# Graph-network kernel: the pairwise stage works in place in the adjacency ring, with 14 slots waited for one by one

## The chip, the cores and the metric

One Trainium2 chip; the kernel runs on one of its cores. The metric is device time in microseconds (us) of one execution, the median over the runs. The times below are from a profiled execution unless a median is named.

## What is computed

Four graph-network layers, each `x = x + f(relu(layernorm(x)), adj)`, for 8 graphs ("batches") of 2048 nodes with 128 features; `adj` is 2048 x 2048 for each. Layer 1 is the one that the change touches:

```python
mask = where(adj > 0, 0, -1e22)
q = feat @ W1.T                                  # 2048 x 64
k = feat @ W2.T                                  # 2048 x 64
e = relu(q[:, None, :, :] + k[:, :, None, :])    # for every pair of nodes, 64 values
scores = einsum('bijd,d->bij', e, a)
att = softmax(scores + mask, axis=-1)
return att @ feat
```

Layer 0 is a three-layer graph convolution, layer 2 attention with four heads, layer 3 a normalised product with the adjacency.

## The kernel before, in words

The five engines' programs are written out by hand: each has its own instruction stream with explicit semaphore waits. The batches run one after the other, and in each the four layers one after the other. The pairwise stage is layer 1.

**A tile and its steps.** The stage has 16 tiles per batch (`tile1`); tile t gives the score rows of 128 nodes. A tile has NS = 15 steps. A step has four "column groups" g = 0..3, and for each of them one slot of the buffer `E` (128 x 2048, float32) is filled: either by DVE (`first`, L881, or `second`, L879), or by ACT (`second`, L611). In steps 4, 6, 8 and 12 one slot is "fused": DVE fills it first and adds a second part to it last (L889). Which engine fills what is fixed by `PLAN`: in a tile, DVE writes 34 slots and makes 4 additions, ACT writes 26 slots. When both engines are done with a step (`e_dve`, `e_act`), PE multiplies the four slots by a window of signs into four PSUM banks (L1361, 32 matmuls for a step) and raises `e_used` by one. The scores of a tile are whole in PSUM after step 14. Tiles alternate between two halves of PSUM, u = t % 2.

**The tail of a tile** runs inside the steps of the next tile, at places fixed in each engine's program:
- DVE, after its step 1: `min1` (L904) waits for the last `e_used` of the tile, adds the mask to the scores, takes the row minimum, and writes the sum to `T1`. After it, DVE waits for its own result (`t1_rdy`, L908) and raises `ring_free` (L910).
- ACT, after its step 3: `exp1` (L616), in place in `T1`.
- PE, after step 5: 16 transposes of `T1` (L1272).
- ACT and DVE, after their step 7: `evac1`, PSUM to `PT1`, two chunks each (L523, L915). `PT1` is another name for `HW`, a buffer of the other layers.
- PE, after step 9: `out1`, the product with the features (128 matmuls, L1376).
- DVE, after its step 11: `finish1`, a reciprocal (L921) and, when `out1` is done, the addition to X (L925); after step 12 `stats2` (L983), after step 13 `mask1_tile` (L896, the mask of the tile made in place from its adjacency) and `aggr2` (L988).

In tiles 5, 9 and 13 there is more: DVE normalises four row blocks after steps 3 to 6 (L996), PE makes four transposes after step 12 (L1414). These are called feature tiles below.

**Slots.** `E` has 12 slots, three steps of four. An engine that begins step n of a batch waits once, for `e_used` of step n - 3.

**The adjacency ring.** `ring` has two places of 128 x 2048. SP loads the adjacency rows of tile k into place k % 2 (L404). For tile k of the pairwise stage it waits for `ring_free`, raised by `min1` of tile k - 2 (L427); for the first two tiles of layer 2 for `min1` of tiles 14 and 15 (L433). SP's queue is in order.

**After the stage** (tile 15 has no next tile) its tail is mixed with the first products of layer 2 (`fill`, `low`, `high`), and `mask2` (L1005) makes the masks of layer 2 from the ring.

Of the kernel before, what the change touches and what calls it, by code (L numbers as in the profile page):

```python
# [52 lines left out]
STEPS = NT * HEADS  # L53


EQ = 3
FUSED = (4, 8, 6, 12)
NS = 2 * SETS - 1
SCALAR_TWO = tuple(k for k in range(NS) if k != 1)
# [28 lines left out]
PLAN = tile_plan()  # L88


def e_slot(t, k):

    return 4 * ((t * NS + k) % EQ)


def k_col(t, g, m):
# [74 lines left out]
def build(nc, x, adj, Ws, bs, gammas, betas, W1, W2, a_vec, Wq, bq, Wk, bk, Wv, bv, Wo, bo, Bw, out):  # L171
# [4 lines left out]
    with ExitStack() as ctx:  # L176
# [73 lines left out]
        with ExitStack() as ph:  # L250
            A = sb("adj_res", [P, NT, N], where=ph)
        with ExitStack() as ph:
            E = sb("E", [P, 4 * EQ, N], where=ph)
            QA = sb("QA", [P, N], where=ph)
            QB = sb("QB", [P, N], where=ph)
            T1 = sb("T1", [P, N], where=ph)
            KLO = sb("KLO", [P, N // GR], where=ph)
            KHI = sb("KHI", [P, N // GR], where=ph)
            KBN = sb("KBN", [P, N // GR], where=ph)
            KBP = sb("KBP", [P, N // GR], where=ph)  # L260
# [4 lines left out]
            T2 = sb("T2", [P, 2, HEADS, N], where=ph)  # L265
            PT2 = sb("PT2", [P, 2, HEADS, CH], where=ph)

        PT1 = HW
        ps = ctx.enter_context(nc.psum_tensor("ps", [P, 8, CH], F32))


# [14 lines left out]
        xn_relu = sem("xn_relu")  # L286
        adj_in = [sem("adj_in0"), sem("adj_in1")]
        ring_in = [sem("ring_in0"), sem("ring_in1")]
        ring_free = sem("ring_free")
        dve_self = sem("dve_self")  # L290
        pool_self = sem("pool_self")
        ln_stats = sem("ln_stats")
# [76 lines left out]
        def _(sp):  # L369
# [48 lines left out]
            for b in range(NB):  # L418

                sp.wait_ge(out_done, b * 16 + 16)  # L420
                for t in range(NT):
                    sp.dma_start(X[:, t, :], x_v[bass.ds(b, 1), :, t].rearrange("o p d -> p (o d)")).then_inc(x_in, 16)
                for k in range(NT):
                    if k < 2 and b:
                        sp.wait_ge(at3_ps, (b * NT + k - 1) * NC)
                    else:
                        sp.wait_ge(ring_free, b * NT + k + 1)  # L427
                    if k == 1:
                        sp.wait_ge(deg_rdy, (b + 1) * NT)
                    load_ring(b, k)  # L430
                for k in range(NT):
                    if k < 2:
                        sp.wait_ge(ring_free, b * NT + NT + k + 1)  # L433
                    else:
                        sp.wait_ge(t2_rdy, b * STEPS + (k - 1) * HEADS)
                    load_ring(b, k)
                    if k == 2:
                        stack_queries(b, 2)
                    if 2 <= k < NT - 1:
                        stack_queries(b, k + 1)  # L440
                for k in range(NT):
                    if k < 2:
                        sp.wait_ge(t2_rdy, b * STEPS + (NT + k - 1) * HEADS)
                    else:
                        sp.wait_ge(at3_ps, (b * NT + k - 1) * NC)
                    load_ring(b, k)
                sp.wait_ge(o3_rdy, b * NT + (2 * NT + 3))
                sp.dma_start(out_v[bass.ds(b, 1)].rearrange("o p t d -> p (o t) d"),
                             X[:, :, :]).then_inc(out_done, 16)
# [71 lines left out]
        def _(act):  # L521
# [80 lines left out]

            def step1(b, t, k):

                n = t * NS + k
                if n >= EQ:
                    act.wait_ge(e_used, b * NT * NS + n - EQ + 1)
                for g, (kind, m, by_act) in enumerate(PLAN[k]):
                    if by_act:
                        col = k_col(t, g, m)  # L610
                        last = nc.scalar.activation(E[:, e_slot(t, k) + g, :], QB[:, :], ACT.Relu, bias=KBP[:, col:col + 1])  # L611
                last.then_inc(e_act, 1)

            def exp1(T, u):
                act.wait_ge(t1_rdy, T + 1)
                nc.scalar.activation(T1[:, :], T1[:, :], ACT.Exp, bias=nmin1[:, u:u + 1], scale=-1.0,  # L616
                                     accum_out=rsum1[:, u:u + 1]).then_inc(p1_rdy, 1)

            def evac1(T, u):
                for g in range(2):  # L620
                    act.wait_ge(pt1_ps, T * NC + g + 1)
                    last = evac(PT1[:, g * CH:(g + 1) * CH], ps[:, 4 * u + g, :])
                last.then_inc(pt1_act, 1)

            def tile1(b, t, u, tail):
# [103 lines left out]
        def _(dve):  # L729
# [5 lines left out]
                own.wait(dve, b)  # L735


            nc.vector.memset(s_win[:, :], 0.0).then_inc(ring_free, 1)
            nc.vector.memset(mv[:, :, :], 0.0).then_inc(ring_free, 1)
            for buf in (stats[:, :, :], dinv[:, :], rstd[:, :]):  # L740
                nc.vector.memset(buf, 0.0).then_inc(cleared, 1)
            dve.wait_ge(ring_free, 2)
            dve.wait_ge(cleared, 3)
            dve.sem_inc(o3_rdy, NT + 3)
            dve.wait_ge(out_done, 16)
            dve.wait_ge(const_in, 16 * CONST_DMAS)
# [119 lines left out]

            def step1(b, t, k):

                n = t * NS + k
                if n >= EQ:  # L870
                    dve.wait_ge(e_used, b * NT * NS + n - EQ + 1)
                add = None
                for g, (kind, m, by_act) in sorted(enumerate(PLAN[k]), key=lambda x: x[1][0] != "fused"):
                    if by_act:
                        continue
                    col = k_col(t, g, m)
                    dst = E[:, e_slot(t, k) + g, :]
                    if kind == "second":
                        last = nc.vector.tensor_scalar(dst, QB[:, :], KBN[:, col:col + 1], None, ALU.max)  # L879
                    else:  # L880
                        last = nc.vector.tensor_scalar(dst, QA[:, :], KLO[:, col:col + 1], KHI[:, col:col + 1], ALU.max, ALU.min)  # L881
                    if kind == "fused":
                        last.then_inc(e_first, 1)
                        add = dst, col
                if add:
                    dst, col = add
                    at = [j for j, row in enumerate(PLAN) if any(kind == "fused" for kind, _, _ in row)].index(k)
                    dve.wait_ge(e_first, (b * NT + t) * 4 + at + 1)
                    last = nc.vector.scalar_tensor_tensor(out=dst, in0=QB[:, :], scalar=KBN[:, col:col + 1], in1=dst,  # L889
                                                          op0=ALU.max, op1=ALU.add)  # L890
                last.then_inc(e_dve, 1)
# [7 lines left out]
            def min1(T, u):  # L899

                dve.wait_ge(e_used, (T + 1) * NS)
                dve.wait_ge(mask1, T + 1)
                alone(dve)
                nc.vector.tensor_tensor_reduce(  # L904
                    out=T1[:, :], in0=ps[:, 4 * u:4 * u + 4, :].rearrange("p c n -> p (c n)"), in1=ring[:, u, :],
                    scale=1.0, scalar=BIG, op0=ALU.add, op1=ALU.min, accum_out=nmin1[:, u:u + 1]
                ).then_inc(t1_rdy, 1)
                dve.wait_ge(t1_rdy, T + 1)  # L908

                dve.sem_inc(ring_free, 1)  # L910

            def evac1(T, u):
                for g in range(2, 4):
                    dve.wait_ge(pt1_ps, T * NC + g + 1)
                    last = nc.vector.tensor_copy(PT1[:, g * CH:(g + 1) * CH], ps[:, 4 * u + g, :])  # L915
                last.then_inc(pt1_dve, 1)

            def finish1(t, T, u):
# [9 lines left out]
            def tile1(b, t, u, tail):  # L928
# [3 lines left out]
                for k in range(NS):  # L932
# [4 lines left out]
                        min1(T - 1, 1 - u)  # L937
                    if tail and k == 7:
                        evac1(T - 1, 1 - u)
                    if tail and k == 11:  # L940
                        finish1(t - 1, T - 1, 1 - u)
                    if k == 13:
                        mask1_tile(b, T, t // 2, u)
                    if t in (5, 9, 13) and 3 <= k < 7:
                        normal2(b, t // 4 - 1, (t - 8 + k,))
                    if tail and k == 12:
                        stats2(b, t - 1)
                    if tail and k == 13:
                        aggr2(b, t - 1)

# [310 lines left out]
        def _(pe):  # L1261
# [85 lines left out]
            def step1(b, t, k, u):  # L1347
# [6 lines left out]
                    pe.wait_ge(x2_rdy, T - 1)  # L1354
                if k == 0 and t in (6, 10, 14):
                    pe.wait_ge(ht_sb, b * (HTS * NC) + NC + t // 4)
                s = e_slot(t, k)
                for c in range(NC):
                    for g, (kind, m, by_act) in enumerate(PLAN[k]):
                        win = s_win[:, QROWS - GR - GR * m:2 * QROWS - GR - GR * m]  # L1360
                        last = mm(ps[QROWS * g:QROWS * (g + 1), 4 * u + c, :], win,  # L1361
                                  E[:, s + g, c * CH:(c + 1) * CH], start=(k == 0), stop=(k == NS - 1),
                                  tile_position=(0, QROWS * g))
                last.then_inc(e_used, 1)

            def probs_t1(T, u):
                pe.wait_ge(p1_rdy, T + 1)
                transposes(lambda t: T1[:, t * P:(t + 1) * P], 4 * u, pt1_ps)

            def out1(T, u):  # L1370
                pe.wait_ge(pt1_act, T + 1)
                pe.wait_ge(pt1_dve, T + 1)
                for j in range(NT):
                    for g in range(NC):
                        rows = slice(QROWS * g, QROWS * (g + 1))
                        last = mm(ps[rows, 4 * u, 0:D], PT1[:, j * P + QROWS * g:j * P + QROWS * (g + 1)], H[:, j, :],  # L1376
                                  start=(j == 0), stop=(j == NT - 1), tile_position=(0, QROWS * g))
                last.then_inc(o1_ps, 1)

# [223 lines left out]
```

## Time and profile before

| | |
|---|---|
| median of 3 runs | 12219.96 us (12218.97 to 12223.52) |
| profiled execution, its own time | 12227.2 us |
| its span | 12225.4 us |
| busy: PE, DVE, ACT | 97%, 84%, 76% |
| DMA, mean over the span | 50 GB/s |
| granted TensorE clock | 0.996 of full speed |

The profile is one execution. Busy time is given for each engine; "idle before" of a group of instructions is the time in which their engine stood still just before them, with what released it. The chain of waits follows the last instruction back to what released it, and so on to the start. A batch takes some 1510 us; its pairwise stage lies, for the second batch, about from 1816 to 2714 us of the span. A matmul's end is modelled; its start is recorded.

### The profile page before, as it was taken

What the parts mean: (1) busy time and instruction counts of PE and PEld (TensorE: products, weight loads), DVE (VectorE), ACT (ScalarE), POOL (GpSimd) and SP (SyncE); (2) the same over time, 40 slices, a digit from 0 to 9 for tenths busy, and PEclk for the clock granted to TensorE, in tenths of its full rate; (3) what the DMA queues carried; (4) which work ended last, traced back from release to release, by engine and by line L of the source; (5) the groups of instructions that cost most, each with busy time, mean ns of one, the idle gap of its engine ahead of it and who ended that gap; (6) DMA issues with size and microseconds to landing.
All of it is one profiled execution on the core that took longest, in us unless ns stands there. A gap on an engine that the chain in (4) does not pass through costs nothing.

```text
span 12225.4 us, 264459 instructions
## 1 busy us (share of the span) xinstructions
PE 11903.6 (97%) x118401; PEld 5910.8 (48%) x118401; DVE 10279.6 (84%) x12373; ACT 9349.5 (76%) x7633; POOL 459.0 (4%) x636
## 2 busy tenths in 40 slices
PE   7999999999999999999999999999999999999999
PEld 3333853338433384333843348433484334843348
DVE  4999849998599975999759997599975999759997
ACT  3998739987499874988748987489874898749986
POOL 1000000000000000000000000000000000000000
PEclk9999999999999999999999999999999999999999
DMA  2000320003200031000310003100031000410013
GB/s 75 19 22 22 107 79 22 19 22 115 74 19 19 26 120 66 19 19 27 130 55 19 19 28 136 48 19 19 31 139 42 19 22 31 141 37 19 22 32 106
DMA packets 206183, 611.30 MB, mean 50 GB/s; under 512 B 45440, under 2 KB 137216, under 8 KB 139520
## 3 DMA queue, kind: packets, MB, share of 16 engines
q1 hardware_dynamic: 184176, 450.72, 10.8%
q0 software_dynamic: 20880, 143.66, 3.2%
q8 instruction: 938, 15.37, 0.5%
q14 instruction: 189, 1.55, 0.0%
HBM read 556.47 MB, written 8.39 MB: 46 GB/s over the span
## 4 chain that ended last, share of the span: by engine, by line
DVE 53%; PE 44%; issue 1%; SPq 1%; ACT 0%; DMA 0%; POOL 0%; DVEq 0%
DVE E L881 34%; PE ps L1341 10%; DVE E L889 9%; PE ps L1361 8%; PE ps L1448 7%; PE ps L1461 4%; PE ps L1521 4%; PE ps L1428 4%; PE ps L1376 3%; DVE T L904 2%; PE ps L1507 2%; DVE E L879 1%; DVE HW L915 1%; DVE adj_ring L896 1%; SPq L415 1%
## 5 line engine op out<-in xcount | busy, mean ns | idle before, releaser
L611 ACT ACTIVATE E<-QB,KBP 128x2048 f32<-128x2048 f32 x3328 | 6398.6, 1994 | 705.6 <-PE ps L1361 691.0
L1361 PE MATMUL ps<-E,s_win 128*32 128x512 f32 x61440 | 6741.2, 594 | 115.3 <-DVE E L889 71.1
L881 DVE TENSOR_SCALAR E<-QA,KLO,KHI 128x2048 f32<-128x2048 f32 x4096 | 5252.2, 1339 | 21.1 <-DVE nmin L904 18.1
L1361 PEld LDWEIGHTS ps<-E,s_win 128*32 128x32 f32 x61440 | 1981.5, 110 | 4672.4 <-issue 4177.4
L1013 DVE CUSTOM_DVE_ANT_0 T<-ps,adj_ring 128x2048 f32<-128x2048 f32 x512 | 1171.8, 2289 | 75.3 <-PE ps L1428 72.0
L889 DVE SCALAR_TENSOR_TENSOR E<-QB,KBN,E 128x2048 f32<-128x2048 f32 x512 | 1200.2, 2344 | 0.0
L643 ACT ACTIVATE T<-T,nmin 128x2048 f32<-128x2048 f32 x512 | 1029.0, 2010 | 183.6 <-DVE nmin L1013 183.6
L1448 PE MATMUL ps<-ident,T 128*128 128x128 f32 x8192 | 1098.9, 276 | 16.9 <-DVE HT L975 12.0
L1448 PEld LDWEIGHTS ps<-ident,T 128*128 128x128 f32 x8192 | 913.5, 141 | 200.5 <-ACT PT L523 71.2
L523 ACT ACTIVATE AGG<-ps 128x512 f32<-128x512 f32 x224 | 126.8, 596 | 1012.5 <-PE ps L1341 980.9
L1341 PE MATMUL ps<-adj_res,H 128*128 128x512 f32 x2048 | 889.5, 592 | 0.0
L523 ACT ACTIVATE PT<-ps 128x512 f32<-128x512 f32 x1536 | 807.3, 594 | 45.8 <-PE ps L1448 38.3
L1428 PE MATMUL ps<-kst,qcur 128*128 128x512 f32 x2048 | 601.6, 415 | 24.4 <-DVE nmin L1013 23.5
L1341 PEld LDWEIGHTS ps<-adj_res,H 128*128 128x128 f32 x2048 | 384.2, 190 | 459.2 <-issue 459.2
L1461 PE MATMUL ps<-PT,V 128*32 128x128 f32 x16384 | 553.4, 276 | 7.0 <-DVE PT L1020 7.0
L829 DVE TENSOR_TENSOR HT<-ps,HW 128x512 f32<-128x512 f32 x64 | 44.0, 687 | 553.5 <-PE ps L1324 553.1
L1376 PEld LDWEIGHTS ps<-H,HW 128*32 128x32 f32 x16384 | 451.9, 110 | 79.6 <-issue 79.6
L1341 PE MATMUL ps<-adj_res,HW 128*128 128x512 f32 x1024 | 446.8, 594 | 31.0 <-DMA adj_res<-in_adj 31.0
L1376 PE MATMUL ps<-H,HW 128*32 128x128 f32 x16384 | 470.9, 273 | 1.4 <-DVE HW L915 1.4
L1020 DVE COPY PT<-ps 128x512 f32<-128x512 f32 x512 | 351.2, 686 | 135.6 <-PE ps L1448 133.8
L1461 PEld LDWEIGHTS ps<-PT,V 128*32 128x32 f32 x16384 | 416.2, 109 | 92.9 <-issue 52.7
L473 POOL TENSOR_TENSOR var<-mv,epses 128x4 f32<-128x4 f32 (+2 forms) x208 | 73.4, 353 | 10136.3 <-DVE mv L988 7527.6
(147 smaller groups left out, 7680.3 us busy)
## 6 DMA issues: line engine op xcount, KB each, us to landing
adj_ring<-in_adj SPq DMA_DIRECT2D x384, 1024.0 KB, 5.0
adj_res<-in_adj POOLq DMA_DIRECT2D x128, 1024.0 KB, 5.9
qcur<-AGG SPq DMA_DIRECT2D x896, 16.0 KB, 2.8
qcur<-HT SPq DMA_DIRECT2D x896, 16.0 KB, 2.2
HW<-in_x POOLq DMA_DIRECT2D x9, 1024.0 KB, 7.1
X<-in_x SPq DMA_DIRECT2D x128, 64.0 KB, 1.9
out_x<-X SPq DMA_DIRECT2D x8, 1024.0 KB, 16.7
wq_r<-in_L_gnn_Wq SPq DMA_DIRECT2D x4, 64.0 KB, 2.3
```

Of the source, the lines that this page charges most:

```text
L523: return nc.scalar.activation(dst, src, ACT.Copy)
L611: last = nc.scalar.activation(E[:, e_slot(t, k) + g, :], QB[:, :], ACT.Relu, bias=KBP[:, col:col + 1])
L643: nc.scalar.activation(T, T, ACT.Exp, bias=nmin2[:, h:h + 1], scale=-1.0, accum_out=rsum2[:, t % 2, h:h + 1]).then_inc(p2_rdy, 1)
L881: last = nc.vector.tensor_scalar(dst, QA[:, :], KLO[:, col:col + 1], KHI[:, col:col + 1], ALU.max, ALU.min)
L889: last = nc.vector.scalar_tensor_tensor(out=dst, in0=QB[:, :], scalar=KBN[:, col:col + 1], in1=dst, op0=ALU.max, op1=ALU.add)
L1013: nc.vector.tensor_tensor_reduce(out=T2[:, t % 2, h, :], in0=ps[:, 4:8, :].rearrange("p c n -> p (c n)"), in1=ring[:, t % 2, :], scale=1.0 ...
L1341: last = mm(ps[:, c, :], src[:, t, :], A[:, t, c * CH:(c + 1) * CH], start=(t == 0), stop=(t == NT - 1))
L1361: last = mm(ps[QROWS * g:QROWS * (g + 1), 4 * u + c, :], win, E[:, s + g, c * CH:(c + 1) * CH], start=(k == 0), stop=(k == NS - 1), tile_p ...
L1376: last = mm(ps[rows, 4 * u, 0:D], PT1[:, j * P + QROWS * g:j * P + QROWS * (g + 1)], H[:, j, :], start=(j == 0), stop=(j == NT - 1), tile_ ...
L1428: last = mm(ps[:, 4 + c, :], qcur[:, t % 4, h, :], kst[:, h, c * CH:(c + 1) * CH], start=True, stop=True)
L1448: last = nc.tensor.transpose(ps[:, bank_of(("probs", q, h)), k * P:(k + 1) * P], T2[:, t % 2, h, j * P:(j + 1) * P], ident[:, :])
L1461: last = mm(ps[HD * h:HD * (h + 1), 3, 0:P], V[:, g * TPC + k, h * HD:(h + 1) * HD], PT2[:, q % 2, h, k * P:(k + 1) * P], start=(g == 0 an ...
```

## The change

- `E` becomes a ring of 14 slots: 13 in `E`, the 14th is `HW`. Slot number i of a batch (i = 4 * step + g) lies at i % 14.
- Each instruction that fills a slot waits by itself, for the step that used the slot last: groups 0 and 1 of step n wait for step n - 4, groups 2 and 3 for step n - 3.
- `T1` and `PT1` are gone: `min1` writes to the ring's place, `exp1` works in place there, the transposes read it, `evac1` writes to it, and `out1` reads it.
- `min1` no longer waits for its own result, and `ring_free` is gone: SP waits for `out1` of tile k - 2 before it loads tile k, and for `out1` of tiles 14 and 15 before the first two loads of layer 2.
- `finish1` comes after DVE's step 12 and `stats2` after step 13, each a step later.

```diff
-EQ = 3
+SLOTS = 14
...
-def e_slot(t, k):
-    return 4 * ((t * NS + k) % EQ)
+def e_slot(t, k, g):
+    return (4 * (t * NS + k) + g) % SLOTS
+def slot_freed(t, k, g):
+    return (4 * (t * NS + k) + g - SLOTS) // 4 + 1
...
-            E = sb("E", [P, 4 * EQ, N], where=ph)
+            E = sb("E", [P, SLOTS - 1, N], where=ph)
-            T1 = sb("T1", [P, N], where=ph)
...
-        PT1 = HW
+        def slot(i):
+            return HW[:, :] if i == SLOTS - 1 else E[:, i, :]
...
@@ SP @@
-                    else:
-                        sp.wait_ge(ring_free, b * NT + k + 1)
+                    elif k >= 2:
+                        sp.wait_ge(o1_ps, b * NT + k - 1)
...
-                        sp.wait_ge(ring_free, b * NT + NT + k + 1)
+                        sp.wait_ge(o1_ps, b * NT + NT + k - 1)
...
@@ ACT, step1 (DVE's has the same edit) @@
-                n = t * NS + k
-                if n >= EQ:
-                    act.wait_ge(e_used, b * NT * NS + n - EQ + 1)
                 for g, (kind, m, by_act) in enumerate(PLAN[k]):
                     if by_act:
+                        freed = slot_freed(t, k, g)
+                        if freed > 0:
+                            act.wait_ge(e_used, b * NT * NS + freed)
...
@@ ACT, exp1 @@
-                nc.scalar.activation(T1[:, :], T1[:, :], ACT.Exp, bias=nmin1[:, u:u + 1], scale=-1.0,
+                nc.scalar.activation(ring[:, u, :], ring[:, u, :], ACT.Exp, bias=nmin1[:, u:u + 1], scale=-1.0,
@@ ACT and DVE, evac1 @@
-                    last = evac(PT1[:, g * CH:(g + 1) * CH], ps[:, 4 * u + g, :])
+                    last = evac(ring[:, u, g * CH:(g + 1) * CH], ps[:, 4 * u + g, :])
...
@@ DVE, min1 @@
-                    out=T1[:, :], in0=ps[:, 4 * u:4 * u + 4, :].rearrange("p c n -> p (c n)"), in1=ring[:, u, :],
+                    out=ring[:, u, :], in0=ps[:, 4 * u:4 * u + 4, :].rearrange("p c n -> p (c n)"), in1=ring[:, u, :],
...
-                dve.wait_ge(t1_rdy, T + 1)
-                dve.sem_inc(ring_free, 1)
...
@@ DVE, tile1 @@
-                    if tail and k == 11:
+                    if tail and k == 12:
                         finish1(t - 1, T - 1, 1 - u)
+                    if tail and k == 13:
+                        stats2(b, t - 1)
                     if k == 13:
                         mask1_tile(b, T, t // 2, u)
...
-                    if tail and k == 12:
-                        stats2(b, t - 1)
...
@@ PE, probs_t1 and out1 @@
-                transposes(lambda t: T1[:, t * P:(t + 1) * P], 4 * u, pt1_ps)
+                transposes(lambda t: ring[:, u, t * P:(t + 1) * P], 4 * u, pt1_ps)
...
-                        last = mm(ps[rows, 4 * u, 0:D], PT1[:, j * P + QROWS * g:j * P + QROWS * (g + 1)], H[:, j, :],
+                        last = mm(ps[rows, 4 * u, 0:D], ring[:, u, j * P + QROWS * g:j * P + QROWS * (g + 1)], H[:, j, :],
```

## Rows read from the trace of the kernel before

**Rows 1.** Page, the chain that ended last: shares of the span by engine.

```profile
DVE 53%; PE 44%; issue 1%; SPq 1%; ACT 0%; DMA 0%; POOL 0%; DVEq 0%
```

**Rows 2.** Windows: busy us (and instructions) of each engine, one tile of batch 1.

```profile
core 0: us, PE busy (x) PEld busy (x) DVE busy (x) ACT busy (x) POOL busy (x), PEclk, DMA share, GB/s
2186.45:2244.59 58.14, 57.57 (x628) 20.79 (x624) 56.95 (x48) 52.74 (x31) 0.00 (x0) 1.00 0.06 19
```

**Rows 3.** Timeline, DVE, the same tile: start, us, instruction, count [idle before <- releaser].

```profile
2186.45 2.29 DVE L904 CUSTOM_DVE_ANT_0 T<-ps,adj_ring 128x2048 f32<-128x2048 f32 x1
...
2188.89 7.63 DVE L881 TENSOR_SCALAR E<-QA,KLO,KHI 128x2048 f32<-128x2048 f32 x6 [0.15 <-DVE nmin L904]
...
2215.73 5.11 DVE L881 TENSOR_SCALAR E<-QA,KLO,KHI 128x2048 f32<-128x2048 f32 x4
...
2225.72 0.15 DVE L921 RECIPROCAL rinv<-rsum 128x1 f32<-128x1 f32 x1
2226.91 0.35 DVE L925 SCALAR_TENSOR_TENSOR X<-ps,rinv,X 128x128 f32<-128x128 f32 x1 [1.04 <-PE ps L1376]
...
2244.59 2.28 DVE L904 CUSTOM_DVE_ANT_0 T<-ps,adj_ring 128x2048 f32<-128x2048 f32 x1
```

**Rows 4.** Timeline, PE, the same tile: steps 6 to 9, out1, step 10 on.

```profile
2208.35 7.07 PE L1361 MATMUL ps<-E,s_win 128*32 128x512 f32 x64
...
2223.09 3.68 PE L1376 MATMUL ps<-H,HW 128*32 128x128 f32 x128
2226.59 38.09 PE L1361 MATMUL ps<-E,s_win 128*32 128x512 f32 x352
```

**Rows 5.** Chain of waits in order of time, same tile: start, us, what.

```profile
2219.63 3.64 PE ps L1361 x32
```

**Rows 6.** Timeline, PE and DVE at the end of tile 15, batch 1.

```profile
2694.63 17.35 PE L1361 MATMUL ps<-E,s_win 128*32 128x512 f32 x160
...
2712.23 2.29 DVE L904 CUSTOM_DVE_ANT_0 T<-ps,adj_ring 128x2048 f32<-128x2048 f32 x1 [5.72 <-PE ps L1361]
```

**Rows 7.** Timeline, DVE behind the stage: the same two operations where nothing is waited for.

```profile
2724.92 0.17 DVE L921 RECIPROCAL rinv<-rsum 128x1 f32<-128x1 f32 x1
2725.12 0.35 DVE L925 SCALAR_TENSOR_TENSOR X<-ps,rinv,X 128x128 f32<-128x128 f32 x1
...
2742.13 2.29 DVE L1013 CUSTOM_DVE_ANT_0 T<-ps,adj_ring 128x2048 f32<-128x2048 f32 x1
...
2744.35 1.28 DVE L958 TENSOR_TENSOR V<-ps,bv_b 128x512 f32<-128x512 f32 x2
```

**Rows 8.** Timeline, PE and DVE in a feature tile, step 10 on.

```profile
2343.91 10.48 PE L1361 MATMUL ps<-E,s_win 128*32 128x512 f32 x96
2354.32 0.66 PE L1414 MATMUL ps<-ident,AGG 128*128 128x128 f32 x4
2354.91 20.38 PE L1361 MATMUL ps<-E,s_win 128*32 128x512 f32 x188
...
2362.33 2.28 DVE L904 CUSTOM_DVE_ANT_0 T<-ps,adj_ring 128x2048 f32<-128x2048 f32 x1
```

**Rows 9.** Groups by line: busy us, mean ns of one, idle before and its releasers.

```profile
L611 ACT ACTIVATE E<-QB,KBP 128x2048 f32<-128x2048 f32 x3328 | 6398.6, 1994 | 705.6 <-PE ps L1361 691.0 <-DVE QB L850 8.1
L889 DVE SCALAR_TENSOR_TENSOR E<-QB,KBN,E 128x2048 f32<-128x2048 f32 x512 | 1200.2, 2344 | 0.0
L879 DVE TENSOR_SCALAR E<-QB,KBN 128x2048 f32<-128x2048 f32 x256 | 327.5, 1279 | 7.8 <-PE ps L1361 7.8
L896 DVE TENSOR_SCALAR adj_ring<-adj_ring 128x2048 f32<-128x2048 f32 x128 | 156.2, 1220 | 0.0
L925 DVE SCALAR_TENSOR_TENSOR X<-ps,rinv,X 128x128 f32<-128x128 f32 x128 | 44.9, 351 | 125.0 <-PE ps L1376 124.8
```

**Rows 10.** Page, DMA issues (median us to landing), and the second mask of layer 2.

```profile
adj_ring<-in_adj SPq DMA_DIRECT2D x384, 1024.0 KB, 5.0
...
2749.47 1.22 DVE L1005 TENSOR_SCALAR adj_ring<-adj_ring 128x2048 f32<-128x2048 f32 x1
```

More of the change, by code:

```diff
@@ L288, in build @@
         ring_in = [sem("ring_in0"), sem("ring_in1")]
-        ring_free = sem("ring_free")
         dve_self = sem("dve_self")
@@ L603, in step1 @@
             def step1(b, t, k):
-                n = t * NS + k
-                if n >= EQ:
-                    act.wait_ge(e_used, b * NT * NS + n - EQ + 1)
                 for g, (kind, m, by_act) in enumerate(PLAN[k]):
                     if by_act:
+                        freed = slot_freed(t, k, g)
+                        if freed > 0:
+                            act.wait_ge(e_used, b * NT * NS + freed)
                         col = k_col(t, g, m)
-                        last = nc.scalar.activation(E[:, e_slot(t, k) + g, :], QB[:, :], ACT.Relu, bias=KBP[:, col:col + 1])
+                        last = nc.scalar.activation(slot(e_slot(t, k, g)), QB[:, :], ACT.Relu, bias=KBP[:, col:col + 1])
                 last.then_inc(e_act, 1)
@@ L735, in link @@
                 own.wait(dve, b)
-            nc.vector.memset(s_win[:, :], 0.0).then_inc(ring_free, 1)
-            nc.vector.memset(mv[:, :, :], 0.0).then_inc(ring_free, 1)
-            for buf in (stats[:, :, :], dinv[:, :], rstd[:, :]):
+            for buf in (s_win[:, :], mv[:, :, :], stats[:, :, :], dinv[:, :], rstd[:, :]):
                 nc.vector.memset(buf, 0.0).then_inc(cleared, 1)
-            dve.wait_ge(ring_free, 2)
-            dve.wait_ge(cleared, 3)
+            dve.wait_ge(cleared, 5)
             dve.sem_inc(o3_rdy, NT + 3)
@@ L867, in step1 @@
             def step1(b, t, k):
-                n = t * NS + k
-                if n >= EQ:
-                    dve.wait_ge(e_used, b * NT * NS + n - EQ + 1)
                 add = None
@@ L875, in step1 @@
                         continue
+                    freed = slot_freed(t, k, g)
+                    if freed > 0:
+                        dve.wait_ge(e_used, b * NT * NS + freed)
                     col = k_col(t, g, m)
-                    dst = E[:, e_slot(t, k) + g, :]
+                    dst = slot(e_slot(t, k, g))
                     if kind == "second":
@@ L914, in evac1 @@
                     dve.wait_ge(pt1_ps, T * NC + g + 1)
-                    last = nc.vector.tensor_copy(PT1[:, g * CH:(g + 1) * CH], ps[:, 4 * u + g, :])
+                    last = nc.vector.tensor_copy(ring[:, u, g * CH:(g + 1) * CH], ps[:, 4 * u + g, :])
                 last.then_inc(pt1_dve, 1)
@@ L1356, in step1 @@
                     pe.wait_ge(ht_sb, b * (HTS * NC) + NC + t // 4)
-                s = e_slot(t, k)
                 for c in range(NC):
@@ L1361, in step1 @@
                         last = mm(ps[QROWS * g:QROWS * (g + 1), 4 * u + c, :], win,
-                                  E[:, s + g, c * CH:(c + 1) * CH], start=(k == 0), stop=(k == NS - 1),
+                                  slot(e_slot(t, k, g))[:, c * CH:(c + 1) * CH], start=(k == 0), stop=(k == NS - 1),
                                   tile_position=(0, QROWS * g))
```

## The prediction

> **What bounds the kernel now.** I read the chain of waits first: 53% of it lies on DVE and 44% on PE [rows 1], so no single engine sets the whole span, and the stage has to be looked at alone. The window of one tile of the pairwise stage, from one `min1` to the next, shows 58.14 us with DVE busy for 56.95, PE for 57.57 and ACT for 52.74 [rows 2]. Two engines are almost full: what is taken from one can give no more than the other lets it. So I read the stage as a loop and follow it by its starts.
>
> The loop before: `min1` starts at 2186.45, and PE's step 9 starts at 2219.63, when DVE has made its third write of that step (the third of the four from 2215.73 on, 1.28 each) [rows 3, 5]. PE then runs step 9 and `out1` and starts step 10 at 2226.59 [rows 4]. DVE has done its reciprocal at 2225.72 and stands for 1.04 us until `out1` is done; it adds to X at 2226.91, and the next `min1` starts at 2244.59, 18.00 us after PE's step 10 [rows 3, 4]. That makes two legs: **from `min1` over DVE to PE's step 10, 40.14 us, and from there over DVE's wait to the next `min1`, 18.00 us.**
>
> The slots bind hardly anything: DVE waited 7.8 us in all for PE before L879, while ACT waited 691.0 us for PE, some 5 us a tile, off the path: with 52.74 of 58.14 us it is not the slowest [rows 2, 9].
>
> **The change part by part.**
>
> *`finish1` a step later.* The reciprocal and the addition start 1.19 us apart where `out1` is waited for, 0.20 apart where it isn't [rows 3, 7]: 0.99 us of DVE's time go away, since DVE's step 12, two writes of 1.27 and an addition of 2.34, some 4.8 us [rows 3, 9], now lies ahead of it and covers the 1.04. `stats2` and `mask1_tile` keep their order behind it and only move along. PE's wait for X before a tile's first step concerns the tile before the last, a dozen steps back, so it stays covered.
>
> What is late next? `min1` also waits for PE's step 14. In tile 15 DVE has nothing else to do and stands there 5.72 us: `min1` starts at 2712.23, 17.60 us after PE's step 10 at 2694.63 [rows 6]. No `min1` can start sooner than that. In the plain tile it starts after 18.00 us; without the wait DVE would be there after 17.01. So the second leg falls from 18.00 to 17.60, a gain of **0.40**, and 0.59 of the 0.99 turns into a new wait before `min1`. In a feature tile PE's three steps and four transposes from 2343.91 to 2354.91 take 11.00 us against 10.3 (three steps of 3.43; five take 17.35 to the end of the last), so the limit is 17.60 + 0.70 = 18.30; `min1` now starts 18.42 after step 10 [rows 6, 8]. Gain **0.12**. In tile 15 it is at the limit already: gain 0.
>
> *The wait after `min1` taken out.* Here 2.44 us lie between `min1`'s start and the next DVE instruction, 0.15 of it shown as idle on its own result [rows 3]. The same kind of operation in layer 2, with no such wait behind it, gives 2.22 [rows 7]. It lies in the first leg, which has DVE up to PE's step 9: **0.22** in each interval. Bounds: 0 (the time belongs to the operation) and 0.22; I take 0.22, since the row is of the same operation with the same shape.
>
> *30 waits more in a tile.* 34 writes of DVE and 26 of ACT each carry a wait, 60 in place of one for each step and engine, 30. What a wait that is already met costs a write: the six writes in a row from 2188.89 on belong to three steps, so three of them carry the old wait, and they take 7.63 us together, 1.27 each; four writes elsewhere 5.11, 1.28 each [rows 3]. So I take 0. From above the bound is the 0.15 of idle time behind `min1` [rows 3]. The new waits are never for a later step than the old ones, so no write can be held longer than now.
>
> *14 slots.* Two groups of four may be written a step earlier. DVE is held for 7.8 us in the whole span [rows 9], all in the leg where PE now sets the end: 0. ACT's waits may shrink; it is off the path. 0 too.
>
> *In place.* `min1` now writes the tile that it reads. Writes in place against others: L896 in place 1220 ns, L879 from another tile 1279; L889, in place with two inputs, 2344 against 2.29 us for `min1` [rows 3, 9]. Bounds of -0.06 and +0.06 us, in the first leg; I take 0. Transposes, `out1` and `evac1` only change the address.
>
> *The ring's loads* start when `out1` is done, 38 us later than after `min1` [rows 3, 4], and land in 5.0 us [rows 10]; the mask for which they come is made more than a tile later (step 13 of tile k, from a load at step 9 of tile k - 1). What covers them is that tile; without it the 5.0 us would lie before `mask1_tile` on DVE. Behind the waiting SP stands only the next load of the ring. At the end of the stage the last `out1` is done by 2725.1, the load would land at 2730, and the mask that needs it comes at 2749.47 [rows 7, 10]: 19 us of cover. 0.
>
> **Sum.** A batch has 15 intervals between its 16 `min1`: 3 of feature tiles, the last one, and 11 plain ones. 11 x (0.40 + 0.22) + 3 x (0.12 + 0.22) + 1 x 0.22 = 6.82 + 1.02 + 0.22 = 8.06 us; for 8 batches **64.5 us**. The rest of the kernel is unchanged. The profiled execution took 12227.2 us, 7 more than the median of 12219.96; I take the gain from the median: 12219.96 - 64.5 = **12155**. (The plain interval falls from 58.14 to 57.52.)
>
> **The rivals.**
>
> *The 0.22 behind `min1` stays.* DVE cannot begin a write while the reading of the accumulator is on its way, wait or no wait. Then 11 x 0.40 + 3 x 0.12 = 4.76 a batch, 38 us, **12182**. Against it: 2.22 in layer 2 [rows 7]. The Trainium skill, "VectorE: DVE Perf Modes", section "The DRAIN you can't avoid", speaks for it: it says that a semaphore behind each operation costs nothing extra, as the pipeline is emptied in any case. The trace does not agree for this operation (2.44 with the wait, 2.22 without), so I give it 8 in 100.
>
> *The full gain.* PE's steps 6 to 9 take 14.74 us from 2208.35 to 2223.09, four steps of at most 3.46 (38.09 / 11) would take 13.85 [rows 4]: PE waits at least 0.89 a tile for DVE. If DVE's lead grew over the tiles so that neither waits for the other, an interval could fall by 0.89: 15 x 8 x 0.89 = 107, **12113**. Against it: step 9 waits for DVE and `min1` for step 14 in each tile, so the lead cannot grow. 7 in 100.
>
> *The wait only moves.* If `min1` could not start sooner after step 10 than it does now, the 0.99 would stand before `min1` whole, and if the 0.22 stayed too, nothing would be gained: **12220**. Against it: the 17.60 of tile 15 [rows 6]. 6 in 100.
>
> *Slower: the new waits cost.* DVE makes 18 writes in steps 2 to 9, with 8 waits now and 18 after, all in the first leg. At 0.15 each [rows 3] that is 1.5 us an interval, 15 x 8 x 1.5 = 180 less 64.5: **12335**. It decides from 0.054 us a wait on (8.06 / 150). Against it: the even spacing above. 5 in 100.
>
> **How the numbers follow.** Forecast 74 in 100, 0.22 stays 8, full gain 7, only moves 6, slower 5. The forecast's own bounds: in place +-0.06 x 120 = +-7 us; the limit of 17.60 from one place, say 0.1 either way, 11 to 12 us; the 0.22 down to 0, 27 us. That gives 12136 to 12190, with the second case in it. I take 12130 to 12192: the full gain, the wait that moves and the slower case are out. This kernel's measurement can tell 0.2%, 24 us, from no change: faster is 74 + 8 + 7 = 0.89, same 0.06, slower 0.05.
>
> **What would show it.** In the new profile: L925 has no idle time that PE ends; L904 gets 0.6 us before it in a plain tile, 0.9 in a feature tile (18.30 - 17.43) and 6.7 at the end of a batch, all released by PE's L1361, 8 x (11 x 0.59 + 3 x 0.87 + 6.71) = 126 us in all; 2.22 from `min1` to the next write; `min1` to `min1` 57.5 in plain tiles, 59.2 in feature tiles; the writes still 1.26 to 1.28 apart. An L904 with no wait before it, or writes further apart, would prove the sum wrong, and so would DVE waits at L896 or L1005 for the ring.

## The result and the profile after

| | median | lowest to highest | runs |
|---|---|---|---|
| before | 12221.74 us | 12218.97 to 12227.46 | 4 |
| after | 12156.39 us | 12155.14 to 12157.42 | 4 |

The ratio is 0.9944, with a 95% interval of 0.9931 to 0.9956: 65 us less, where the sum had 64.5 and the forecast was 12155. That the time came within 1.4 us of the forecast is in part luck: the median of the kernel before lies between 12219.96 and 12227.75 us from one group of runs to another. So times of different groups are compared below by their ratios to the kernel before, or by the intervals in the traces. The profiled execution of the changed kernel took 12155.14 us, its span is 12153.3.

First the chain that ended last, by engine and by line (it answers to [rows 1]):

```profile
PE 58%; DVE 40%; issue 1%; SPq 1%; ACT 0%; DMA 0%; POOL 0%; DVEq 0%
DVE E L884 24%; PE ps L1360 21%; PE ps L1341 11%; PE ps L1447 8%; DVE E L892 7%; PE ps L1460 4%; PE ps L1520 4%; PE ps L1427 4%; PE ps L1375 3%; DVE adj_ring L907 2%; PE ps L1506 2%; DVE HW L884 2%; DVE adj_ring L915 1%; PE ps L1324 1%; DVE T L1013 1%
```

DVE had 53% of the chain and has 40; PE's steps (L1360, before L1361) had 8% and have 21. Before, the chain went from `out1` over DVE's addition to X and DVE's steps 12 to 14 to the next `min1`; now it goes on from `out1` over PE's steps 10 to 14. The chain of one tile in order of time (start, us, what; the lines left out are DVE's writes between; `DVEq L368` is DVE's instruction that waits for PE) shows that:

```profile
2175.98 2.29 DVE adj_ring L907
2178.27 0.01 DVE nmin L907
2178.28 7.55 DVE E L884 x6
...
2205.11 3.78 DVE E L884 x3
2208.90 0.04 issue
2208.94 3.64 PE ps L1360 x32
2212.58 3.49 PE ps L1375 x128
2216.07 17.21 PE ps L1360 x160
2233.28 0.03 issue
2233.31 0.05 DVEq L368
2233.36 0.13 issue
2233.49 2.29 DVE adj_ring L907
```

This is the loop of the prediction: from `min1` (L907) over DVE's steps 2 to 9, 32.96 us, to PE's step 9 at 2208.94; from there over step 9, `out1` (L1375) and steps 10 to 14 to the next `min1`. From `min1` to `min1` it is 57.51 us, where [rows 2, 3] had 58.14. The timeline of the same tile, DVE and the start of PE's step 10 (the chain puts that at 2216.07, the modelled end of `out1`; the start in the timeline is recorded):

```profile
2175.98 2.29 DVE L907 CUSTOM_DVE_ANT_0 adj_ring<-ps,adj_ring 128x2048 f32<-128x2048 f32 x1 [0.50 <-PE ps L1360]
2178.19 0.08 DVE L907 DVE_READ_ACCUMULATOR2_ANT nmin<- 128x1 f32 x1
2178.19 7.63 DVE L884 TENSOR_SCALAR E<-QA,KLO,KHI 128x2048 f32<-128x2048 f32 x6
...
2205.03 5.12 DVE L884 TENSOR_SCALAR E<-QA,KLO,KHI 128x2048 f32<-128x2048 f32 x4
...
2215.89 0.59 PE L1360 MATMUL ps<-E,s_win 128*32 128x512 f32 x1
...
2219.79 0.17 DVE L921 RECIPROCAL rinv<-rsum 128x1 f32<-128x1 f32 x1
2219.99 0.35 DVE L925 SCALAR_TENSOR_TENSOR X<-ps,rinv,X 128x128 f32<-128x128 f32 x1
...
2233.49 2.29 DVE L907 CUSTOM_DVE_ANT_0 adj_ring<-ps,adj_ring 128x2048 f32<-128x2048 f32 x1 [0.50 <-PE ps L1360]
```

Reciprocal and addition are 0.20 us apart, not 1.19; the next write begins 2.21 us after `min1`, not 2.44 [rows 3]; and `min1` waits 0.50 us for PE, 17.60 us after PE's step 10, where in this tile it had no wait at all. Over the whole span (groups by line; busy us, mean ns, idle before and its releaser):

```profile
L907 DVE CUSTOM_DVE_ANT_0 adj_ring<-ps,adj_ring 128x2048 f32<-128x2048 f32 x128 | 293.5, 2293 | 122.7 <-PE ps L1360 122.7
L882 DVE TENSOR_SCALAR E<-QB,KBN 128x2048 f32<-128x2048 f32 x224 | 288.7, 1289 | 0.0
L899 DVE TENSOR_SCALAR adj_ring<-adj_ring 128x2048 f32<-128x2048 f32 x128 | 155.2, 1213 | 0.0
L925 DVE SCALAR_TENSOR_TENSOR X<-ps,rinv,X 128x128 f32<-128x128 f32 x128 | 45.0, 351 | 4.5
```

The 125.0 us before L925 [rows 9] are 4.5 now, none of it released by PE; 122.7 us stand before `min1`, against 126 foretold, and the 7.8 us before L879 (now L882) are gone.

### The profile page after: what moved, and what is told of

Read it like the earlier page. It is cut to its first block, busy times and chain, and to the rows that moved or that the text cites. A ratio compares the mean times of both kernels' runs of the same rounds, so it can differ in the third digit from the quotient of the medians.

```text
span 12153.3 us, 264330 instructions
## 1 busy us (share of the span) xinstructions
PE 11870.1 (98%) x118401; PEld 5913.5 (49%) x118401; DVE 10281.0 (85%) x12373; ACT 9318.2 (77%) x7633; POOL 459.3 (4%) x636
## 4 chain that ended last, share of the span: by engine, by line
PE 58%; DVE 40%; issue 1%; SPq 1%; ACT 0%; DMA 0%; POOL 0%; DVEq 0%
DVE E L884 24%; PE ps L1360 21%; PE ps L1341 11%; PE ps L1447 8%; DVE E L892 7%; PE ps L1460 4%; PE ps L1520 4%; PE ps L1427 4%; PE ps L1375 3%; DVE adj_ring L907 2%; PE ps L1506 2%; DVE HW L884 2%; DVE adj_ring L915 1%; PE ps L1324 1%; DVE T L1013 1%
## 5 line engine op out<-in xcount | busy, mean ns | idle before, releaser
L1360 PE MATMUL ps<-E,s_win 128*32 128x512 f32 x57088 | 6715.2, 594 | 73.1 <-DVE E L892 26.0
L617 ACT ACTIVATE E<-QB,KBP 128x2048 f32<-128x2048 f32 x3104 | 5961.3, 1997 | 669.5 <-PE ps L1360 661.4
L884 DVE TENSOR_SCALAR E<-QA,KLO,KHI 128x2048 f32<-128x2048 f32 x3808 | 4906.9, 1347 | 3.9
L1360 PEld LDWEIGHTS ps<-E,s_win 128*32 128x32 f32 x57088 | 1979.1, 110 | 4593.1 <-issue 4273.1
L1360 PE MATMUL ps<-HW,s_win 128*32 128x512 f32 x4352 | 1959.6, 593 | 0.0
L892 DVE SCALAR_TENSOR_TENSOR E<-QB,KBN,E 128x2048 f32<-128x2048 f32 x472 | 1110.5, 2353 | 0.0
L1375 PEld LDWEIGHTS ps<-H,adj_ring 128*32 128x32 f32 x16384 | 451.9, 110 | 79.6 <-issue 79.6
L1375 PE MATMUL ps<-H,adj_ring 128*32 128x128 f32 x16384 | 470.8, 273 | 1.4 <-DVE adj_ring L915 1.4
L1360 PEld LDWEIGHTS ps<-HW,s_win 128*32 128x32 f32 x4352 | 466.0, 110 | 0.0
```

The costliest lines, as they stand in the source:

```text
L617: last = nc.scalar.activation(slot(e_slot(t, k, g)), QB[:, :], ACT.Relu, bias=KBP[:, col:col + 1])
L1375: last = mm(ps[rows, 4 * u, 0:D], ring[:, u, j * P + QROWS * g:j * P + QROWS * (g + 1)], H[:, j, :], start=(j == 0), stop=(j == NT - 1), t ...
```

## The experiments

Two theories were to be told apart, and each has a rival. **Two legs:** an interval is a leg that DVE sets (`min1` to PE's step 10) and a leg that PE sets (step 10 to the next `min1`), so 0.22 comes from the first and, in plain tiles, 0.40 of 0.99 from the second. Its rival is DVE's own sum. **The slots carry nothing** was a term of the sum; its rival is that the freer ring makes the gain. The intervals below are from `min1` to `min1` in the trace of each kernel; a batch has 11 plain ones, 3 of feature tiles, and the last. Before: 58.14, 59.59, 57.74. After: 57.51, 59.26, 57.51.

### One part alone: `finish1` a step later (e1)

```diff
-                    if tail and k == 11:
+                    if tail and k == 12:
                         finish1(t - 1, T - 1, 1 - u)
+                    if tail and k == 13:
+                        stats2(b, t - 1)
...
-                    if tail and k == 12:
-                        stats2(b, t - 1)
```

> The kernel before with one edit: finish1 after step 12 and stats2 after step 13; 12 slots, T1 and the wait behind min1 stay. Theory (two legs; min1 cannot start sooner than PE's step 14 allows): plain interval between two min1 58.14 - 0.40 = 57.74, feature tiles - 0.12, 12182 us. The same theory with the slots counted: with 12 of them DVE's first write of step 1 waits for PE's step 13, which held it for 0.33 us in the tile after a feature tile, and then min1 starts 17.72 us after PE's step 10, not 17.60: plain interval 57.86, feature tiles unchanged, 12195 us. Rival (DVE's own sum sets the interval): 0.99 us in each of 15 x 8 intervals, 12101 us.

Measured: 12197.47 us, before 12225.82 on the same chip, ratio 0.9977 (0.9968 to 0.9987). Intervals 57.84, 59.60, 57.74. Timeline of DVE:

```profile
2181.41 2.28 DVE L904 CUSTOM_DVE_ANT_0 T<-ps,adj_ring 128x2048 f32<-128x2048 f32 x1
...
2235.54 1.29 DVE L879 TENSOR_SCALAR E<-QB,KBN 128x2048 f32<-128x2048 f32 x1 [0.60 <-PE ps L1361]
2236.74 2.60 DVE L881 TENSOR_SCALAR E<-QA,KLO,KHI 128x2048 f32<-128x2048 f32 x2
2239.26 2.28 DVE L904 CUSTOM_DVE_ANT_0 T<-ps,adj_ring 128x2048 f32<-128x2048 f32 x1
```

DVE's own sum is out: it would have given 119 us, and 28 came. The wait did not go to `min1` but to the write three places ahead of it, 0.60 us before L879: with 12 slots this first write of step 1 has to wait for PE's step 13, and `min1` comes 3.72 us after it, 17.70 us after PE's step 10. That is the second form of the theory, with the slots counted.

In the feature tiles the move alone brings nothing, 59.60 where it was 59.59. The same write, first in the kernel before and then in this one:

```profile
2358.61 1.29 DVE L879 TENSOR_SCALAR E<-QB,KBN 128x2048 f32<-128x2048 f32 x1 [0.33 <-PE ps L1361]
...
2352.99 1.29 DVE L879 TENSOR_SCALAR E<-QB,KBN 128x2048 f32<-128x2048 f32 x1 [1.32 <-PE ps L1361]
```

It waited there already in the kernel before, since PE makes its four transposes ahead of step 13, and the whole 0.99 us went into that wait.

### The other part alone: no wait behind `min1` (e2)

```diff
-                dve.wait_ge(t1_rdy, T + 1)
-                dve.sem_inc(ring_free, 1)
...
-                    else:
-                        sp.wait_ge(ring_free, b * NT + k + 1)
+                    elif k >= 2:
+                        sp.wait_ge(t1_rdy, b * NT + k - 1)
...
-                        sp.wait_ge(ring_free, b * NT + NT + k + 1)
+                        sp.wait_ge(t1_rdy, b * NT + NT + k - 1)
```

(the start-up lines that set `ring_free` are changed with it)

> The kernel before with one edit: no wait of DVE for its own result behind min1; SP waits for min1's own semaphore in place of ring_free. Theory: 2.44 us from min1 to the next write become 2.22, in the leg that DVE sets; every interval 0.22 shorter, 15 x 8 x 0.22 = 26 us, 12194 us. Rival (the time belongs to the operation, wait or not): 12220 us, 2.44 stays.

Measured: 12196.91 us, before 12225.82, ratio 0.9976 (0.9966 to 0.9985). Intervals 57.91, 59.36, 57.51. Timeline of DVE:

```profile
2183.76 2.29 DVE L900 CUSTOM_DVE_ANT_0 T<-ps,adj_ring 128x2048 f32<-128x2048 f32 x1
2185.97 0.08 DVE L900 DVE_READ_ACCUMULATOR2_ANT nmin<- 128x1 f32 x1
2185.97 7.63 DVE L877 TENSOR_SCALAR E<-QA,KLO,KHI 128x2048 f32<-128x2048 f32 x6
```

The next write begins 2.21 us after `min1`, and each kind of interval is 0.23 shorter, also in the feature tiles and the last one, where the later `finish1` alone brought nothing. It acts in the first leg.

### The wait put back into the changed kernel (e5)

```diff
                 ).then_inc(t1_rdy, 1)
+                dve.wait_ge(t1_rdy, T + 1)
+                alone(dve)
```

> The changed kernel with DVE's wait for its own result put back behind min1. Theory: 0.22 us more in each of 15 x 8 intervals, 26 us, 12183 us. Rival (the pipeline is emptied in any case, the wait costs nothing): 12156 us.

Measured: 12187.48 us, before 12225.57, ratio 0.9970 (0.9958 to 0.9982). Intervals 57.75, 59.51, 57.75. Timeline of DVE:

```profile
2180.50 2.29 DVE L907 CUSTOM_DVE_ANT_0 adj_ring<-ps,adj_ring 128x2048 f32<-128x2048 f32 x1 [0.51 <-PE ps L1362]
2182.72 0.08 DVE L907 DVE_READ_ACCUMULATOR2_ANT nmin<- 128x1 f32 x1
2182.95 7.63 DVE L884 TENSOR_SCALAR E<-QA,KLO,KHI 128x2048 f32<-128x2048 f32 x6 [0.15 <-DVE nmin L907]
```

The write begins 2.45 us after `min1` again, and the interval is 0.24 longer. With e2 this settles the price from both sides: the wait costs 0.23 to 0.24 us, where the two rows of before said 0.22. The Trainium skill ("VectorE: DVE Perf Modes", "The DRAIN you can't avoid") says of eight `tensor_copy` that a semaphore after each costs nothing extra. `min1` raises `t1_rdy` with this edit and without it; what costs time here is DVE's wait for it, and for such a wait that sentence gives no price.

### 12 slots (e3)

```diff
-SLOTS = 14
+SLOTS = 12
```

> The changed kernel with 12 slots in place of 14, waits still one by one. The prediction's term for the slots was 0: 12156 us. Theory with the slots counted: the first write of step 1 waits for PE's step 13 again, min1 starts 17.72 us after PE's step 10 in place of 17.60, 0.12 us in 14 of 15 intervals, 14 x 8 x 0.12 = 13 us, 12170 us, and L882 shows the wait. Rival (the freer ring carries the gain): back to near 12195 us or more.

Measured: 12167.42 us, before 12225.82, ratio 0.9951 (0.9937 to 0.9966). The ratio's interval overlaps that of the change; the trace decides: 57.60, 59.36, 57.51, so 0.09 to 0.10 us more in 14 of 15 intervals, 8 x (11 x 0.09 + 3 x 0.10) = 10 us. Timeline of DVE:

```profile
2178.74 2.29 DVE L907 CUSTOM_DVE_ANT_0 adj_ring<-ps,adj_ring 128x2048 f32<-128x2048 f32 x1
...
2232.64 1.29 DVE L882 TENSOR_SCALAR E<-QB,KBN 128x2048 f32<-128x2048 f32 x1 [0.60 <-PE ps L1360]
2236.35 2.29 DVE L907 CUSTOM_DVE_ANT_0 adj_ring<-ps,adj_ring 128x2048 f32<-128x2048 f32 x1
```

The same 0.60 us as in e1. So the slots do carry something: in plain tiles not a wait that was there before, but one that the earlier arrival of DVE would have run into; in feature tiles the wait at L879 that was there (e1). This kernel differs from before by e1, e2, the writing in place and the waits one by one; e1 and e2 together would give 57.84 - 0.23 = 57.61. In place and one by one thus cost nothing that can be seen in the intervals.

### `finish1` back in its place (e4)

```diff
-                    if tail and k == 12:
+                    if tail and k == 11:
                         finish1(t - 1, T - 1, 1 - u)
```

(and `stats2` after step 12 again)

> The changed kernel with finish1 after step 11 and stats2 after step 12 again; 14 slots, in place, no wait behind min1. Theory: L925 waits 1.0 us for out1 again, the second leg is 18.00 us again in plain tiles; what is left of the gain is 0.22 in 15 intervals and 0.12 in 3, 3.66 x 8 = 29 us, 12191 us. Rival (DVE's own sum): 0.99 x 15 x 8 = 119 us more than after the change, 12275 us. Rival (slots carry the gain): 12156 us.

Measured: 12194.78 us, before 12225.82, ratio 0.9974 (0.9964 to 0.9984). Intervals 57.91, 59.27, 57.51. Group by line, and `min1` at the end of a feature interval:

```profile
L925 DVE SCALAR_TENSOR_TENSOR X<-ps,rinv,X 128x128 f32<-128x128 f32 x128 | 44.9, 351 | 124.4 <-PE ps L1375 124.1
...
2358.40 2.29 DVE L907 CUSTOM_DVE_ANT_0 adj_ring<-ps,adj_ring 128x2048 f32<-128x2048 f32 x1 [0.24 <-PE ps L1360]
```

14 slots, in place, and no wait behind `min1`, and the plain interval is that of e2. The freer ring alone gives nothing there; the wait at L925 is whole again. In the feature tiles it does give something, 59.27 against 59.36 in e2: without the wait at L879, `min1` reaches PE's limit, 18.32 us after step 10, even with the wait at L925. So the gain of the second leg in feature tiles belongs to the slots, with or without the later `finish1`.

### A second wait before every write of DVE (e8)

```diff
                         dve.wait_ge(e_used, b * NT * NS + freed)
+                    dve.wait_ge(k1_sb, b * 2 + 1)
```

> The changed kernel with a second wait, for a semaphore that has long had its value, in front of each of DVE's 34 writes of a tile: two waits do not go into one instruction, so this adds instructions that only wait. Theory (a wait that is met costs nothing): 12156 us, writes 1.26 us apart. Rival (each costs DVE time): at 0.05 us each 18 of them lie in the leg that DVE sets, 0.9 us in 15 x 8 intervals, 108 us, 12264 us.

Measured: 12156.86 us, before 12225.57, ratio 0.9946 (0.9931 to 0.9961). Intervals 57.51, 59.27, 57.51. The trace has 5262 instructions on DVE that only wait or count, where the changed kernel has 966. Timeline of DVE:

```profile
2174.95 2.29 DVE L908 CUSTOM_DVE_ANT_0 adj_ring<-ps,adj_ring 128x2048 f32<-128x2048 f32 x1 [0.50 <-PE ps L1361]
2177.17 0.08 DVE L908 DVE_READ_ACCUMULATOR2_ANT nmin<- 128x1 f32 x1
2177.17 7.63 DVE L885 TENSOR_SCALAR E<-QA,KLO,KHI 128x2048 f32<-128x2048 f32 x6
```

Six writes, each behind an instruction of its own that waits, take the same 7.63 us. The slower rival falls: a wait that is already met costs DVE nothing here, be it carried by the write or standing in front of it.

### Where the new wait goes: `min1` after step 2 (e6), and `exp1` after step 4 (e7)

```diff
-                    if tail and k == 1:
+                    if tail and k == 2:
                         min1(T - 1, 1 - u)
```

> The changed kernel with min1 after DVE's step 2 in place of step 1. Theory: the loop that sets the interval crosses from PE to DVE at min1, where DVE now stands for 0.50 us; two writes later PE's step 14 is done and DVE no longer waits there, so the loop is cut. Then PE alone sets the interval: 57.51 less what it still waits for DVE in steps 8 and 9, some 57.1 to 57.2 in plain tiles and 57.9 in feature tiles, 11 x 0.36 + 3 x 1.3 = 7.9 us a batch, 12093 us. Rival (the wait comes back at another place, at a slot or at exp1): 12156 us or more.

Measured: 12094.60 us, before 12225.57, ratio 0.9896 (0.9879 to 0.9912). Intervals 57.18 in plain tiles (56.93 in the first three of a batch), 58.16 in feature tiles. Window of one interval and the chain by line from 2100 to 2280 us:

```profile
core 0: us, PE busy (x) PEld busy (x) DVE busy (x) ACT busy (x) POOL busy (x), PEclk, DMA share, GB/s
2165.37:2222.56 57.19, 57.19 (x632) 20.94 (x625) 57.00 (x49) 52.43 (x31) 0.00 (x0) 1.00 0.06 20
```

```profile
by line: PE ps L1360 88.3%; PE ps L1375 5.8%; PE ps L1272 3.2%; DVE E L884 2.7%; DVE adj_ring L907 1.2%; issue 0.2%
```

PE is busy for the whole interval, and the chain stays on PE through the plain tiles. There the loop between the two engines is cut, at the place where the change had put its wait. In feature tiles the chain still goes over DVE (here from 2274.70 to 2311.16 us), and they come to 58.16, not to the 57.9 expected; the first three intervals of a batch, 56.93, make up for most of that, so the time agrees better than its terms.

```diff
-                    if tail and k == 3:
+                    if tail and k == 4:
                         exp1(T - 1, 1 - u)
```

> As the one before, and exp1 after ACT's step 4 in place of step 3. Theory: where PE alone sets the interval, its step 4 waits some 0.1 us for ACT's pair of writes that stands behind exp1; with exp1 a step later this goes too, 15 x 8 x 0.1 = 12 us, 12081 us. Rival (exp1 ends too late for the transposes, or PE does not wait there): the same as the one before, 12093 us, or more.

(the edit of e6 is in it too.) Measured: 12087.94 us, before 12225.57, ratio 0.9889 (0.9874 to 0.9904). Timeline of DVE:

```profile
2110.44 2.28 DVE L907 CUSTOM_DVE_ANT_0 adj_ring<-ps,adj_ring 128x2048 f32<-128x2048 f32 x1
...
2167.47 2.28 DVE L907 CUSTOM_DVE_ANT_0 adj_ring<-ps,adj_ring 128x2048 f32<-128x2048 f32 x1
...
2224.49 2.28 DVE L907 CUSTOM_DVE_ANT_0 adj_ring<-ps,adj_ring 128x2048 f32<-128x2048 f32 x1
```

57.03 in plain tiles, 0.15 less (56.91 in the first four of a batch, of which three had 56.93 before); the feature tiles stay at 58.16. From the first to the last `min1` of a batch it is 1.50 us less, 12 us in all. That is the sum that was foretold, but not its terms: 0.1 was expected in each of 15 intervals, and nine have it, with 0.15 and more. The median moved by 7 only, and the two intervals of the ratio overlap; outside these stretches the profiled execution took 6.7 us more than that of e6, and whether that comes from the edit isn't shown. So the trace bears the gain in the plain tiles out, and the time does not prove it. This is the fastest version, some 68 us below the change.

### The same edit without the change, and without the slots (e9, e10)

The edit of e6 in the kernel before:

> The kernel before with one edit: min1 after DVE's step 2 in place of step 1. Theory: before the change DVE did not wait at min1 but at finish1, for out1; the loop goes from there over min1 and steps 2 to 9 back to out1, and holds the same work in either order: interval 58.14, 12221 us, L925 still waits 1.0 us. Rival (a later min1 frees DVE by itself, as after the change): some 60 us less, 12160 us.

Measured: 12227.21 us, before 12227.75, ratio 1.0000 (0.9990 to 1.0009). Intervals 58.15, 59.60. Group by line:

```profile
L925 DVE SCALAR_TENSOR_TENSOR X<-ps,rinv,X 128x128 f32<-128x128 f32 x128 | 45.0, 351 | 124.9 <-PE ps L1376 124.6
```

The edit of e6 and `SLOTS = 12` in the changed kernel:

> The changed kernel with min1 after step 2 and 12 slots in place of 14. Theory: DVE now waits for PE at the first write of step 1 (its slot comes free with PE's step 13), at the same point of the loop as with min1 after step 1; the loop has the same work, 57.60 in plain and 59.36 in feature tiles as with 12 slots alone, 12167 us: with 14 slots this wait is for step 12, and the 14 slots are then worth some 70 us where they were worth 11. Rival (the slots are worth little in either order): 12105 us.

Measured: 12169.10 us, before 12227.75, ratio 0.9954 (0.9939 to 0.9969). Intervals 57.60, 59.36. Group by line:

```profile
L882 DVE TENSOR_SCALAR E<-QB,KBN 128x2048 f32<-128x2048 f32 x256 | 328.6, 1284 | 84.7 <-PE ps L1360 84.7
```

Moving `min1` is worth nothing until the wait ahead of it is gone. In the kernel before DVE stands at L925 in either order. With 12 slots DVE stands at L882, ahead of `min1` in either order, and moving `min1` changes no interval; with 14 the same move is worth some 60 us (ratios 0.9944 and 0.9896). The two slots were worth 10 us with `min1` after step 1, and are worth some 70 with it after step 2.

## Why the prediction was right

*The loop.* From PE's step 10 to the next `min1` the trace of after has 17.60 us in plain tiles (18.01 before), 18.32 in feature tiles (18.42) and 17.60 in the last (17.60). The limit read from a single place, the end of tile 15 [rows 6], held in every tile. From `min1` to step 10 it has 39.91 where it had 40.14. Both legs came out within 0.02 us of their terms, and the intervals within 0.01: 57.51, 59.26 and 57.51 against 57.52, 59.25 and 57.52.

*`finish1`.* In plain tiles the 0.99 us went as foretold, and 0.59 of it came back before `min1`. In the trace 0.50 is shown as idle: the rest, some 0.1, is hidden by the way idle time is counted, from the end of the operation before. Where `min1` does not wait, it begins 0.08 us ahead of that end (in e1 at 2239.26, where the writes from 2236.74 on take 2.60).

*The wait behind `min1`.* 0.22 from two rows of the same operation; 0.23 and 0.24 by e2 and e5. The sentence of the Trainium skill that the prediction held against these rows is about a semaphore that is raised, and the term is about one that is waited for (e5).

*30 waits more* and *in place* cost nothing that can be seen (e8 for DVE's waits; e3 for both). L907 in place takes 2293 ns on the mean, 10 more than L904, but in e3 it takes 2286 in place, as L904 does in e1 not in place; the bounds were -0.06 and +0.06 us.

*The ring's loads.* No wait on them: L899, the mask of the pairwise stage, has 0.0 us before it (as L896 before, [rows 9]), and L1005, the mask behind the stage, waits for loads 1.4 us in the whole span, 1.6 before.

*The slots: the one term that was mis-sized.* The step "DVE is held for 7.8 us in the whole span [rows 9], all in the leg where PE now sets the end: 0" was wrong by 10 us (e3). In plain tiles it counted only the waits that were there. But the term of 0.40 took for granted that DVE reaches `min1` unhindered, and with 12 slots it would not have: moved up by 0.99 us, its first write of step 1 runs into PE's step 13, and 0.30 is left of the 0.40 (e1). In feature tiles the 7.8 us themselves lay on the path, 0.33 us in each of 24 tiles, and the gain there was put to the wrong part: of the 0.12 that the prediction gave to the later `finish1`, the move alone brought nothing (e1), and the slots alone brought the 0.10 that came (e4). The sum came out right because the 14 slots were in the change, and so in its terms, without being named; on the kernel before, the same move is worth 28 us (e1), not the 38 of its terms. The row that told it was there: L879's 7.8 us, all in the tiles after a feature tile, where PE's four transposes put step 13 back.

*The range.* Its bounds were 7 us for writing in place, 12 for the limit and 27 for the 0.22. Upwards all three together give 12201, not the 12190 of the prediction, which leaves the 12 out. The measured time lies inside with either.

*The rivals.* The full gain fell (an engine waits for the other once a tile, as argued, and nothing grew); it did come, and went beyond 12113, once `min1` was moved (e6): the 0.89 us in which PE waited could be had, and the plain interval fell by 0.96 in all, from 58.14 to 57.18. That the 0.22 stays fell by e2 and e5, the slower case by e8, that the wait only moves by the result itself.

## What to carry to other kernels

Where two engines are both nearly full, look for the loop that crosses from one to the other, write down its legs from one engine's start to the other's, and price an edit in the leg where it lies: 0.99 us of DVE's waiting was worth 0.40 in a plain tile, since PE was next, 0.41 us behind, and nothing in a feature tile. The limit of the next wait can be read where the program lets an engine come early, here at the end of a batch. A buffer that nobody waits for today can be what an earlier arrival would wait for: try the edit with and without it.

## What the runs showed of the hardware that was not expected

4296 more instructions on DVE that only wait, one in front of nearly every write of the stage, cost no time: 7.63 us for six writes with and without them (e8). A wait of DVE for the result of its own operation with accumulator (`min1`), in contrast, costs 0.23 to 0.24 us each time (e2, e5); by e8 it is not the instruction that waits which costs this, but the waiting.
